# FP4 weight staging spread over the first batch, and FFN weights loaded through transposing DMAs, in an attention plus FFN layer on eight cores

## What is computed

```python
def fp4_quant_dequant(x):                 # blocks of 16 along the last dim
    xb = x.reshape(shape[:-1] + (shape[-1] // 16, 16))
    scale = jnp.maximum(jnp.max(jnp.abs(xb), -1, keepdims=True) / 6.0, 1e-12)
    q = _GRID[jnp.searchsorted(_MID, jnp.abs(xb / scale))] * jnp.sign(xb) * scale
    return q.reshape(shape)
def fp4_linear(x, w):                     # both operands are rounded
    return jnp.einsum('bsk,nk->bsn', fp4_quant_dequant(x), fp4_quant_dequant(w))

xn  = _layernorm(x)
attn = causal_attention(xn, WQ, WK, WV, WO)          # 16 heads of 64, seq 2048
ffn = fp4_linear(silu(fp4_linear(xn, w_gate)) * fp4_linear(xn, w_up), w_down)
out = x + attn + ffn                                  # w_gate, w_up: [2816, 1024]; w_down: [1024, 2816]
```

## Time and profile before

| | us |
|---|---|
| median of 2 runs (8909.17 and 9041.93) | 8975.55 |
| the profiled execution | 8907.39 |
| its span on the slowest core, first to last instruction | 8905.8 |
| spans of the 8 cores | 8868.8 to 8905.8 |
| one sequence after the first (4973 to 6939) | 1966 |
| PE busy / DVE busy / ACT busy / POOL busy | 5248.8 / 3172.5 / 2391.8 / 2268.4 |

### The profile page before, as it was taken

How to read it: one execution, slowest core, us unless ns; L and a number is a source line. 1 busy time by engine, 2 the same in 40 slices (tenths; PEclk the granted TensorE clock), 3 DMA queues, 4 the chain that set the end, 5 groups by cost and what they waited for, 6 DMA issues and landing times.

```text
span 8905.8 us, 81694 instructions; the slowest of 8 cores (8868.8 to 8905.8 us)
## 1 busy us (share of the span) xinstructions
PE 5248.8 (59%) x21392; PEld 2152.5 (24%) x21392; DVE 3172.5 (36%) x5268; ACT 2391.8 (27%) x4112; POOL 2268.4 (25%) x2237
## 2 busy tenths in 40 slices
PE   0000147665777547665777457666777366656777
PEld 0000013111333222112333222112333122112333
DVE  2444460001466550001666540001666530002665
ACT  0000133551111234551111234550111235541111
POOL 0334321110233221110343221110333211110433
PEclk9999968666888668766888677657888677667888
DMA  4222200002100100002100100002010100011000
GB/s 128 55 59 61 75 26 10 1 1 78 71 36 36 57 22 10 1 1 97 59 36 36 55 20 8 1 27 108 29 36 36 52 22 1 1 63 71 36 36 36
DMA packets 137330, 354.95 MB, mean 40 GB/s; under 512 B 76352, under 2 KB 77376, under 8 KB 132160
## 3 DMA queue, kind: packets, MB, share of 16 engines
q1 hardware_dynamic: 135488, 347.64, 11.4%
q10 hardware_dynamic: 1408, 2.10, 0.1%
HBM read 255.85 MB, written 93.85 MB: 39 GB/s over the span
## 4 chain that ended last, share of the span: by engine, by line
PE 38%; DVE 25%; issue 11%; ACT 11%; DMA 8%; POOL 6%; DVEq 1%; SPq 0%; ACTq 0%; POOLq 0%
PE ps_c L610 10%; DVE heap L235 4%; ACT heap L597 4%; DVE heap L226 4%; POOL heap L604 3%; DVE heap L257 3%; PE ps_a L790 3%; PE ps_a L582 3%; DVE heap L229 3%; PE ps_c L697 3%; PE ps_a L548 3%; PE ps_b L548 2%; PE ps_a L732 2%; DVE heap L238 2%; DVE heap L810 2%
## 5 line engine op out<-in xcount | busy, mean ns | idle before, releaser
L245 POOL TENSOR_TENSOR heap<-heap 128x512 f32<-128x512 f32 (+3 forms) x564 | 914.2, 1621 | 3955.4 <-DVE heap L241 3955.4
L610 PE MATMUL ps_c<-heap 128*65 128x512 bf16 (+3 forms) x2560 | 1083.3, 458 | 797.2 <-POOL heap L604 369.0
L623 DVE CAST heap<-ps_c 64x512 bf16<-64x512 f32 x256 | 174.9, 683 | 2658.5 <-PE ps_c L610 2617.2
L604 POOL TENSOR_TENSOR heap<-heap,tri 128x128 bf16<-128x128 bf16 x1024 | 435.7, 425 | 2392.6 <-ACT heap L597 2281.4
L597 ACT ACTIVATE heap<-ps_a 128x512 bf16<-128x512 f32 (+1 forms) x1280 | 640.4, 552 | 744.1 <-PE ps_a L582 717.5
L247 POOL TENSOR_TENSOR heap<-heap 128x512 f32<-128x512 f32 (+3 forms) x564 | 764.5, 1356 | 81.7 <-POOL heap L245 1.3
L840 PE MATMUL ps_c<-heap 128*128 128x512 bf16 x2816 | 717.8, 422 | 5.0 <-ACT heap L874 5.0
L610 PEld LDWEIGHTS ps_c<-heap 128*65 128x65 bf16 x2560 | 312.2, 122 | 1672.1 <-issue 1659.6
L226 DVE TENSOR_REDUCE heap<-heap 128x32 f32<-128x512 f32 (+3 forms) x564 | 412.4, 731 | 505.3 <-DMA heap<-w_up 165.5
L597 ACT ACTIVATE heap<-ps_b 128x512 bf16<-128x512 f32 (+2 forms) x1280 | 592.0, 527 | 0.0
L235 DVE TENSOR_TENSOR heap<-heap 128x512 f32<-128x512 f32 (+3 forms) x564 | 501.3, 889 | 60.9 <-DVE heap L232 2.8
(11 more groups left out here) (78 smaller groups left out, 6158.0 us busy)
## 6 DMA issues: line engine op xcount, KB each, us to landing
heap<-x SPq DMA_DIRECT2D x128, 512.0 KB, 3.4
attn_scr<-heap SPq DMA_DIRECT2D x64, 512.0 KB, 2.6
heap<-attn_scr SPq DMA_DIRECT2D x64, 512.0 KB
out<-heap SPq DMA_DIRECT2D x64, 512.0 KB, 2.7
heap<-wg_d SPq DMA_DIRECT2D x4, 5632.0 KB, 21.1
heap<-wu_d SPq DMA_DIRECT2D x4, 5632.0 KB, 37.6
heap<-wd_d SPq DMA_DIRECT2D x4, 5632.0 KB
heap<-w_gate SPq DMA_DIRECT2D x22, 512.0 KB, 4.2
```

Source lines behind the costliest of these rows:

```text
L245: P.emit("gpsimd", lambda e: e.tensor_tensor(u, u, M, op=ALU.add), waits=[(s_ve, ve_m), (s_po, s_po.n)], inc=(s_po, 1))
L604: P.emit("gpsimd", lambda e, eb=eb: e.tensor_tensor(eb[:, 0:128], eb[:, 0:128], tri[:], op=ALU.mult), waits=[(s_ac, ac_exp), (s_po, s_po.n ...
L610: pr=pr, s_=s_, vst=vst, jm=jmax: e.matmul(pv[:, off:off + n], vst[:, j, pr * 2 + s_, 0:65], eb[:, 0:n], start=(j == 0), stop=(j == jm - 1)),
```

## The change

It does four things, in one diff.

1. `wg_d`, `wu_d` and `wd_d` keep the weights' own orientation ([2816, 1024], [2816, 1024], [1024, 2816]); the PE transposes, ACT copies and 256-byte writes of the staging are gone.
2. The staging ahead of the first sequence is gone. The same weights are cut into 68 chunks: 22 + 22 of [128, 1024], then 8 times 1024, 1024 and 768 columns of `w_down`. A new function `pump_wq()` emits one chunk: load, two halves of at most 512 columns each through `quant_pre` and `quant_deq`, write. It has one staging buffer, one scratch set and a semaphore `s_wq` of its own; the load waits for everything emitted on `s_wq` and on DVE.
3. `pump_wq()` is called in the first sequence only: twice in each of the 16 layernorm tiles, once behind each of the 32 groups of the Q and K projections, three times behind each pair of heads. So 32 + 32 chunks are emitted before attention, 3 behind the first pair and 1 behind the second.
4. The three loads per sequence become transposing DMAs: 8 for gate, 8 for up, each [2816, 128] of HBM to [128, 2816], and 22 for down, each [1024, 128] to [128, 1024]. Read from HBM this is a row of 256 bytes at a time.

```diff
-        pend = None
+        wq_chunks = []
         for win, wout in ((wg_in, wg_d), (wu_in, wu_d)):
             for ic in range(NI):
-                wp = wk_i % 2
...
+                wq_chunks.append((win, wout, ic * 128, 0, D))
         for c in range(NCD):
...
+            for p0, plen in ((0, 1024), (1024, 1024), (2048, 768)):
+                wq_chunks.append((wd_in, wd_d, c * 128, p0, plen))
+        wq_state = {"i": 0, "bfrd": [0, 0]}
+
+        def pump_wq():
...
+            wp = k % 2
+            stg = vf(WQ_STG, plen)
+            stgb = vb(WQ_BF[wp], plen)
+            P.emit("sync", lambda e, win=win, r0=r0, p0=p0, plen=plen, stg=stg: e.dma_start(
+                out=stg, in_=win[r0:r0 + 128, p0:p0 + plen]),
+                waits=[(s_wq, s_wq.n), (s_ve, s_ve.n)], inc=(s_wq, 16))
+            P.wait("vector", [(s_wq, s_wq.n), (s_wq, wq_state["bfrd"][wp])])
+            for hh in range(0, plen, 512):
+                hl = min(512, plen - hh)
+                tok = quant_pre(stg[:, hh:hh + hl], WQ_U, WQ_M, WQ_QS, hl)
+                quant_deq(tok, stgb[:, hh:hh + hl], hl)
+            ve_q = s_ve.n
+            P.emit("sync", lambda e, wout=wout, r0=r0, p0=p0, plen=plen, stgb=stgb: e.dma_start(
+                out=wout[r0:r0 + 128, p0:p0 + plen], in_=stgb),
+                waits=[(s_ve, ve_q)], inc=(s_wq, 16))
+            wq_state["bfrd"][wp] = s_wq.n
...
                 ac_vevac = s_ac.n
+                if b == 0:
+                    pump_wq()
+                    pump_wq()
...
                         evac_of_buf[bi] = s_ac.n
+                        if b == 0:
+                            pump_wq()
...
+                if b == 0:
+                    pump_wq()
+                    pump_wq()
+                    pump_wq()
             pe_attn_done = s_pe.n
...
-            P.emit("sync", lambda e, wgq=wgq: e.dma_start(out=wgq, in_=wg_d[:]),
-                   waits=[(s_ws, ws_stageW), (s_w, s_w.n)], inc=(s_w, 16))
...
+            ws_w = ws_stageW_final()
+            for c in range(NCD):
+                P.emit("sync", lambda e, c=c, wgq=wgq: e.dma_start_transpose(
+                    wgq[:, c, :], wg_d[:, c * 128:(c + 1) * 128]),
+                    waits=([(s_wq, ws_w), (s_w, s_w.n)] if c == 0 else []), inc=(s_w, 16))
...
-            P.emit("sync", lambda e, wdq=wdq: e.dma_start(out=wdq, in_=wd_d[:]),
-                   waits=[(s_ws, ws_stageW), (s_pe, pe_outproj_done)], inc=(s_sc2, 16))
+            for it in range(NI):
+                P.emit("sync", lambda e, it=it, wdq=wdq: e.dma_start_transpose(
+                    wdq[:, it, :], wd_d[:, it * 128:(it + 1) * 128]),
```

More of the change, by code:

```diff
@@ L84, in build_core_program @@
     wo_d = nc.dram_tensor("wo_d", [128, NCD, D], BF16, kind="Internal").ap()
-    wg_d = nc.dram_tensor("wg_d", [128, NCD, I], BF16, kind="Internal").ap()
-    wu_d = nc.dram_tensor("wu_d", [128, NCD, I], BF16, kind="Internal").ap()
-    wd_d = nc.dram_tensor("wd_d", [128, NI, D], BF16, kind="Internal").ap()
+    wg_d = nc.dram_tensor("wg_d", [I, D], BF16, kind="Internal").ap()
+    wu_d = nc.dram_tensor("wu_d", [I, D], BF16, kind="Internal").ap()
+    wd_d = nc.dram_tensor("wd_d", [D, I], BF16, kind="Internal").ap()
     es = ExitStack()
@@ L192, in build_core_program @@
         s_zg = [Sem(es, nc, "s_zg0"), Sem(es, nc, "s_zg1")]
+        s_wq = Sem(es, nc, "s_wq")
         s_st = Sem(es, nc, "s_st")
@@ L198, in build_core_program @@
         s_po = Sem(es, nc, "s_po")
-        ALL = (s_x, s_w, s_sc, s_sc2, s_zg[0], s_zg[1], s_st, s_ws, s_pe, s_ve, s_ac, s_po)
+        ALL = (s_x, s_w, s_sc, s_sc2, s_zg[0], s_zg[1], s_wq, s_st, s_ws, s_pe,
+               s_ve, s_ac, s_po)
         P = Prog()
@@ L296, in build_core_program @@
         P.wait("vector", [(s_ws, ws_attnW)])
[L298 to L316, removed]
@@ L332, in build_core_program @@
[L332 to L357, removed]
@@ L375, in build_core_program, with ws_stageW_final @@
+        ws_stageW_v = [None]
+        def ws_stageW_final():
+            while wq_state["i"] < len(wq_chunks):
+                pump_wq()
+            if ws_stageW_v[0] is None:
+                ws_stageW_v[0] = s_wq.n
+            return ws_stageW_v[0]
         for b in range(NB):
@@ L649, in build_core_program @@
             wuq = vb(F_WU, NCD * I).rearrange("p (c i) -> p c i", i=I)
-            P.emit("sync", lambda e, wgq=wgq: e.dma_start(out=wgq, in_=wg_d[:]),
-                   waits=[(s_ws, ws_stageW), (s_w, s_w.n)], inc=(s_w, 16))
-            P.emit("sync", lambda e, wuq=wuq: e.dma_start(out=wuq, in_=wu_d[:]),
-                   inc=(s_w, 16))
+            ws_w = ws_stageW_final()
[3 more added lines that the diff above has]
+                    waits=([(s_wq, ws_w), (s_w, s_w.n)] if c == 0 else []), inc=(s_w, 16))
+            for c in range(NCD):
+                P.emit("sync", lambda e, c=c, wuq=wuq: e.dma_start_transpose(
+                    wuq[:, c, :], wu_d[:, c * 128:(c + 1) * 128]),
+                    inc=(s_w, 16))
             w_gu_ld = s_w.n
@@ L752, in build_core_program @@
             wdq = vb(F_WD, NI * D).rearrange("p (t n) -> p t n", n=D)
-            P.emit("sync", lambda e, wdq=wdq: e.dma_start(out=wdq, in_=wd_d[:]),
-                   waits=[(s_ws, ws_stageW), (s_pe, pe_outproj_done)], inc=(s_sc2, 16))
+            for it in range(NI):
+                P.emit("sync", lambda e, it=it, wdq=wdq: e.dma_start_transpose(
+                    wdq[:, it, :], wd_d[:, it * 128:(it + 1) * 128]),
+                    waits=([(s_wq, ws_stageW_final()), (s_pe, pe_outproj_done)]
+                           if it == 0 else []),
+                    inc=(s_sc2, 16))
             w_d_ld = s_sc2.n
```

46 lines of the change are left out of this document (15 added, 31 removed).

## The result

The changed kernel takes 9140.62 us (median of 11 executions, 9131.05 to 9216.08), the kernel before 8922.1 (median of 10). The ratio is 1.0261 with a 95% interval of 1.0228 to 1.0293: 2.6% slower, where 9250 and 3.8% were forecast.

A forecast was written before the change was run, and what follows sets the result against it. In-order DVE and POOL dependences were taken as the bound, with DVE free only in attention. 8907.4 + 375 (staging) - 38 (rz_d) = 9244, say 9250 us; own range 9150 to 9350, whole range 9140 to 10,700.

The forecast's parts named there:

- Removed, 873 us: FFN staging ahead of the first sequence: its start moves from 1042.45 to 169.7 us, 873 us removed.
- One chunk, 20.8 and 18.2 us: Two halves, 14.1 us, plus load 4.1 and write 2.6: 20.8 us behind another chunk, 18.2 behind other DVE work.
- staging sum: First sequence: exposed chunks in layernorm, Q and K, and attention, less the removed staging: 650 + 528 + 70 - 873 = +375 us.
- Layernorm, +650: Layernorm loop, first sequence: 32 chunks uncovered, 624 us, plus 26 us for the later x tile: 650 added.
- Q and K, +528: Q and K projections: 32 chunks take 654 us, 126 covered by PE and ACT work before the first mask; 528 exposed.
- Attention, +70: First attention: three chunks behind the first pair expose 56 us, one behind the second 14; 70 in all.
- The cover: First sequence: DVE's free time lies in attention, not where chunks land; the staging's only real cover is 126 us.
- Rival B: Chunks in the first sequence overlap at 13.9 us each: 8830 us, no measurable change; decides at about 15 us; chance 0.04.
- Rival C: Attention covers more: POOL's masks not held, 16 chunks behind K beside attention, 330 us gained, 8920; chance 0.02.
- The transposing DMAs, nothing exposed: FFN weight loads: gate and up 56 us under 135 of cover, down 28 under 70; 0 exposed.
- Rival A: Transposing FFN weight loads outlast their covers: 10,520 us at 6.2 times the packet price; decides at 2.4 times; chance 0.36.
- rz_d, -38: Softmax sums: rz_d's write, 22.75 us beside the bulk load, gets quicker; gain between 0 and 76 us, half taken.

The follow-up runs named there:

- e3: Changed kernel with two staging buffers, so the next chunk's load is issued early: 8797.84 us, 343 us under the changed kernel.
- e4: Changed kernel with all 68 chunks emitted ahead of the first sequence: 9294.22 us, 154 us over the changed kernel.
- e5: Changed kernel with 8 chunks moved to one per pair of heads, ahead of its last query chunk: 9011.28 us, 129 us under the changed kernel.
- e1: Changed kernel with plain bulk loads of wg_d, wu_d and wd_d in place of the transposing DMAs: 9326.39 us, ratio 1.0443 to the kernel before.
- e2: Kernel before with wg_d and wu_d loaded by 8 plain DMAs each, rows of 5632 bytes in place of 45,056: 8892.4 us, ratio 0.9952.
- e6: Changed kernel's layout and transposing loads, but staging ahead of the first sequence in two-deep slices, nothing spread: 8648.19 us, ratio 0.9692 to the kernel before.
- e7: As e6, with the next slice's load issued ahead of the write of the one before: 8529.3 us, ratio 0.9543 to the kernel before.

## Why the prediction was right, and where it was off

The time was forecast at 9250 with a range of its own of 9150 to 9350, inside a whole range from 9140. The measured 9140.62 is 9 us under the first and 0.6 above the second: the direction and the mechanism were right, but that the time still lies inside the whole range, by 0.6 us, is luck. The two terms that were mis-sized, the DMA part of a chunk and the gain on rz_d, both err to the slow side and do not hide each other; the range allowed 0.3 us on a chunk and half the bounds of rz_d, where 0.7 to 1.0 and nearly the whole were needed.

- **Removed, 873 us.** Right: the first sequence starts at 164.91 where it started at 1038.46 on core 1, 873.6 us.
- **One chunk, 20.8 and 18.2 us.** The 7.07 us of dependent DVE and POOL work in a half hold to a hundredth. The DMA part was too large: load to first use is 3.3 to 3.6 us, not 4.1, and the write 2.0 to 2.2, not 2.6. I had read both from the attention-weight staging, where SP issues each load within 0.5 us of the write of the slice before, so that the two run beside each other; in a chunk each is alone. That this is why they are shorter is argued, not tested. A full chunk behind another takes 19.8 us in the layernorm loop and 20.0 in Q and K in place of 20.8, one behind other work some 17.5 in place of 18.2; over the 64 chunks ahead of attention that is 52 of the 56 us by which the staging sum is too large. e3 takes this part away and gains what it should.
- **Layernorm, +650.** Measured 912 against 295: +617. **Q and K, +528.** From the write of the last chunk of the layernorm loop to the first mask 632 us, less 126: +506. **Attention, +70.** 649.4 us from the first mask to the end against 578.9: +70.5. Net +320 by these, +318.7 by the end of attention; forecast +375.
- **The cover.** The step that said DVE's free time is in attention and the chunks are not placed there is what e4 and e5 test: 133 us of 1325 covered, and a chunk in the right place free. Rival B (chunks overlap after all) needed 15 us a chunk and falls with the 19.6 us of the profile. Rival C (the masks not held back) falls with the first mask 0.14 us behind POOL's last step of chunk 64, and with the copies 63.3 us apart around three chunks.
- **The transposing DMAs, nothing exposed.** Right. At 20 ns a row 56 us were worked out for gate and up. The 68 us from 2384 on core 1, and what comes behind them:

```profile
2384.00:2452.00 68.00, 39.53 (x43) 12.64 (x44) 13.96 (x11) 0.00 (x0) 0.00 (x0) 0.50 0.97 175
2452.00:2480.00 28.00, 20.29 (x22) 5.89 (x21) 6.11 (x5) 0.00 (x0) 0.00 (x0) 0.50 0.00 1
```

  The DMA engines are busy 0.97 of the time, which is 0.97 x 68 x 16 / 45,056 = 23 ns a row, and then idle. So gate and up have landed before 2452, and the writes of attn_scr start at 2486.66: nothing waits. For down, from the issue of wd_d to the start of the next sequence it is 732.2 us and was 732.6 (core 1), so nothing is exposed there either. Rival A (they outlast their covers), which held 0.36, falls. The Trainium skill gives 1309 ns per 128x128 tile ("VectorE: DVE Perf Modes", section The three transpose paths), by which the 352 tiles one after another would be 461 us, an estimate. About 66 us were taken, so in this long stream it is no price per tile. The Trainium skill's 261 GB/s ("DMA: Bandwidth & Descriptors", section Latency and other measured facts) is above the 175 measured here; both leave the loads inside their cover.
- **rz_d, -38.** Mis-sized by my halving: 79 us on core 1 (24.2 + 54.6), just over my upper bound of 76. 59 of them are the write itself (79.6 us in four sequences before, 20.5 now); most of the rest is the read of rz_d behind it, in the same chain, for which I had no term. The direction of the mechanism (the small packets wait for long rows) was right, as e1 and e2 show, and with short rows nearly the whole wait goes, not half. It is also what I should have seen as a free gain for the kernel before.

Sum: 9244, the forecast before it was rounded, - 56 (staging) - 41 (rz_d) = 9147. The forecast started from the slowest core; core 1 was 10.5 us shorter before, which makes 9136.5 against the 9136.8 measured on it.

## What to carry to other kernels

Work moved into a loop costs nothing only if each engine and queue it uses, in order, is not due for anything before it is through: look for the next mask, copy and load behind it, not for a low busy share (the layernorm loop's DVE was busy 62% and had no room at the end of a tile; attention's had gaps of 20 to 28 us in known places). When a bulk load runs beside small DMAs on another queue, try shorter rows: beside 45 KB rows a 128 KB write took 20.9 us in the median, beside 5.6 KB rows 7.4. And judge the parts of a change apart: here one part was worth 3% alone and was buried under another.

## What the runs showed of the hardware that was not expected

- A tensor-tensor product of 128x1024 fp32 on DVE with both inputs in SBUF took 1.23 us alone and 2.75 when POOL's tensor-tensor had begun 0.67 us before it (e6 against e7), so that it ended 1.08 us after POOL's did. A tensor-scalar of 128x64 took 0.82 in place of 0.20 and ended with POOL's L253, while the reduction L234 (1.22) and the reciprocal L240 (0.55) took beside POOL what they took without it. Together this set the 8.49 us of a slice.
- A transposing DMA of [2816, 128] holds SP for 2.8 to 4.9 us (31.84 us for 8), one of [1024, 128] for 1.1 to 2.5 (31.62 for 22). Whatever else SP has to issue stands behind that; here it had nothing due.
- A low mean granted clock need not mean slow matmuls. In the Q and K window of core 1 the mean is 0.57, but PE's groups of 16 matmuls took 3.62 us there as in the kernel before, where the mean was 0.97. The low mean is that of the waits: from 1120 to 1415, without one matmul, the clock stood at 0.50, the lower of its two levels (1.2 GHz), and with PE at work from 1094 to 1110 at 1.00. What a wait cost was the first group behind it, 5.41 us in place of 3.62 after 307.79 us, and 5.57 in the kernel before after only 8.07.
- PE without work does not always stand at the lower level: ahead of the first matmul the clock was 1.00 (and 1290 us long in e4), and also in the FFN staging of the kernel before, with PE busy for 41 of 568 us. What makes it fall is not shown here.
